# Softmax denominators of a cross-attention kernel: the context's share summed on TensorE, four rear pieces instead of five, a new order on every engine

## The reference, cut to what matters

```python
def layernorm(x, g, b): ...            # mean and variance over the last axis
def rmsnorm(x, gamma):
    norm = sqrt(sum(x * x)) * x.shape[-1] ** -0.5
    return x / maximum(norm, RMS_EPS) * gamma

# cross attention: x is (4, 512, 128), context (4, 77, 96), 2 heads of 64
lat = layernorm(_layernorm(x)); xn = layernorm(context)
q  = lat @ Wq.T
kv = concatenate([xn @ Wkv.T, lat @ Wlkv.T], axis=1)   # 77 context keys, then 512 of its own
attn = softmax(mask(rmsnorm(q) * SCALE @ rmsnorm(k).T))
x = x + (attn @ v) @ Wo.T + bo

# mixture of 8 experts, the best 2 of each token
l = _layernorm(x)
gates = softmax(l @ Wg + bg)
x = x + sum over the top 2 of gates * (l @ W[e] + b[e])
```

## Time and profile before

| what | value |
|---|---|
| median of three runs | 121.44 us (121.33 to 122.02) |
| profiled execution: time, span | 120.44 us, 118.6 us |
| PE busy | 105.5 us, 89% of the span |
| POOL busy | 92.3 us, 78% |
| ACT busy | 85.9 us, 72% |
| DVE busy | 79.4 us, 67% |
| PEld busy | 74.5 us, 63% |
| mean granted TensorE clock | 0.971 |

### The profile page before, as it was taken

One profiled execution on the slowest core, in us unless ns is written; L12 is line 12 of the kernel. 1 busy time (PEld: TensorE's weight loads), 2 busy tenths in 40 slices (PEclk: granted clock), 3 DMA queues, 4 the chain that ended last, 5 costly groups with the idle time before them and its releaser, 6 DMA issues.

```text
span 118.6 us, 2507 instructions
## 1 busy us (share of the span) xinstructions
PE 105.5 (89%) x733; PEld 74.5 (63%) x733; DVE 79.4 (67%) x317; ACT 85.9 (72%) x209; POOL 92.3 (78%) x113
## 2 busy tenths in 40 slices
PE   4999988999999989999999989999999999797500
PEld 4999877673487654654284577677578867485300
DVE  0541599302287572597209559999999999999990
ACT  0327878789898995799685799695969593597600
POOL 3570479999999999959986659949169899879982
PEclk9999998699999999999999999999999999999995
DMA  3616951000000000000000000000000110110112
GB/s 101 149 15 182 343 102 34 0 0 3 0 0 0 7 0 0 6 3 0 0 0 0 0 6 0 0 8 3 0 0 12 37 44 6 38 47 0 44 44 88
DMA packets 6679, 3.92 MB, mean 33 GB/s; under 512 B 2314, under 2 KB 6282, under 8 KB 6667
## 3 DMA queue, kind: packets, MB, share of 16 engines
q1 hardware_dynamic: 5835, 3.41, 10.4%
q10 hardware_dynamic: 832, 0.36, 1.1%
HBM read 2.72 MB, written 1.05 MB: 32 GB/s over the span
## 4 chain that ended last, share of the span: by engine, by line
POOL 38%; PE 27%; DVE 18%; issue 11%; ACT 3%; POOLq 1%; DVEq 0%; ACTq 0%
PE PS L923 8%; DVE part L892 6%; PE PS L1068 6%; POOL esum L421 5%; PE PS L1047 5%; POOL rq L396 4%; POOL e L430 4%; POOL xbo L442 4%; POOL rk L402 3%; POOL rstd L388 3%; PE PS L1102 2%; DVE acc L892 2%; POOL pair L473 2%; POOL rstd L450 2%; POOL We L378 2%
## 5 line engine op out<-in xcount | busy, mean ns | idle before, releaser
L602 ACT ACTIVATE probs<-PS,shift,rk 128x512 f32<-128x512 f32 (+1 forms) x40 | 25.0, 694 | 4.6 <-PE PS L1047 4.4
L660 ACT ACTIVATE scaled<-PS,w 128x128 f32<-128x128 f32 x64 | 17.4, 385 | 4.6 <-PE PS L916 3.7
L1068 PE MATMUL PS<-probs,V_sb 128*64 128x512 f32 (+1 forms) x80 | 16.1, 519 | 0.0
L914 PE MATMUL PS<-WeH,l2H 128*128 128x512 f32 x32 | 13.5, 423 | 1.8 <-ACT scaled L660 0.9
L473 POOL TENSOR_TENSOR pair<-scaled 128x512 f32<-128x512 f32 x8 | 10.3, 1286 | 4.0 <-ACT scaled L660 3.6
L916 PE MATMUL PS<-WeH,l2L 128*128 128x512 f32 x32 | 12.6, 393 | 0.0
L915 PE MATMUL PS<-WeL,l2H 128*128 128x512 f32 x32 | 12.5, 391 | 0.0
L430 POOL TENSOR_TENSOR e<-probs,probs 128x1024 f32<-128x1024 f32 (+1 forms) x5 | 9.7, 1931 | 3.0 <-ACT probs L602 3.0
L421 POOL TENSOR_TENSOR esum<-probs,probs 128x1024 f32<-128x1024 f32 (+1 forms) x5 | 10.7, 2141 | 1.1 <-ACT probs L602 1.1
L923 PE MATMUL PS<-ident 128*128 128x128 f32 x60 | 9.4, 324 | 1.5 <-POOL ident L366 1.5
L1047 PE MATMUL PS<-QH,KH 64*128 64x512 f32 (+1 forms) x40 | 9.0, 435 | 1.3 <-DVE QL L773 0.7
(11 more groups left out here) (144 smaller groups left out, 280.8 us busy)
## 6 DMA issues: line engine op xcount, KB each, us to landing
out_dram<-x SPq DMA_DIRECT2D x8, 128.0 KB, 1.7
x_sb<-in_x_dram SPq DMA_DIRECT2D x3, 256.0 KB, 5.5
We_sb<-in_L_ffn_W_dram SPq DMA_DIRECT2D x1, 512.0 KB, 5.3
We_end<-in_L_ffn_W_dram SPq DMA_DIRECT2D x1, 512.0 KB, 8.9
x_sb<-in_x_dram SPq DMA_DIRECT2D x2, 128.0 KB, 2.5
Wlkv_sb<-in_L_xattn_Wlkv_dram ACTq DMA_DIRECT2D x1, 128.0 KB, 3.0
ctx_sb<-in_ctx_dram SPq DMA_DIRECT2D x1, 115.5 KB
Wkv_sb<-in_L_xattn_Wkv_dram ACTq DMA_DIRECT2D x1, 96.0 KB, 2.8
```

The lines of the kernel that those rows point to most:

```text
L602: act.activation(probs[p % 2][n][:, h, s], ps[:, s], ACT.Exp, bias=shift[:, 0:1], scale=rk[:, b, n, h:h + 1]).then_inc(probs_made, 1)
L660: last = act.activation(scaled[m // 2 % 2][:, m % 2, e], ps[:, e], ACT.Copy, scale=w[:, m, e:e + 1])
L914: pe.matmul(dst, lH, rH, start=True, stop=False)
L1068: last = pe.matmul(bank("value", p, 0)[h * D:(h + 1) * D, s], v, pr, start=(n == 0), stop=(n == KT - 1))
```

## The change

It does six things.

1. `esum2` goes. `den` now has eight products: four with the sum of key tiles 0 to 3, and four with the context's 77 rows of `probs`, which accumulate into the same PSUM columns. `esum1` becomes `esum`. `den` waits for the context's exponentials itself, and the `exp` of piece p, for p from 2 on, also waits for the `den` of piece p-2, since that now reads the buffer.
2. `REAR` has four pieces: batch 3 is done whole.
3. The warm-up transposes go from 60 to 24 (14, 1, 4, 4, 1).
4. `logits_` reads the logits from PSUM for the difference `lgs`, and makes `two` by a reduction over one element instead of a copy.
5. `cbias_` works in the PSUM bank, without `mbias`.
6. All four tables are new: the order of the jobs on every engine and the banks.

```diff
-REAR = ((0, 0, 4), (1, 0, 4), (2, 0, 4), (3, 0, 2), (3, 2, 4))
+REAR = ((0, 0, 4), (1, 0, 4), (2, 0, 4), (3, 0, 4))
...
 TENSOR = """
-    warm 0 35 7   weights 0 0 0   warm 1 3 7   weights2 0 0 1   warm 2 11 7   xT 0 0 2   warm 3 11 7   q 0 0 3
+    warm 0 14 7   weights 0 0 0   warm 1 1 7   weights2 0 0 1   warm 2 4 7   xT 0 0 2   warm 3 4 7   q 0 0 3
...
                 if p >= 2 and n == 0:
 
                     act.wait_ge(O_done, p - 1)
+                    act.wait_ge(den_done, p - 1)
                     act.wait_ge(esum_made, p - 1)
...
-            def esum1_(p, n):
+            def esum_(p, n):
 
                 s = slice(0, (REAR[p][2] - REAR[p][1]) * P)
                 dve.wait_ge(e01_made, p + 1)
                 dve.wait_ge(e23_made, p + 1)
-                step(dve.tensor_tensor(esum[p % 2][:, :, s], esum[p % 2][:, :, s], e23[:, :, s], ALU.add))
-
-            def esum2_(p, n):
-
-                s = slice(0, (REAR[p][2] - REAR[p][1]) * P)
-                dve.wait_ge(dve_step, count[0])
-                dve.wait_ge(probs_made, H * KT * (p + 1))
-                dve.tensor_tensor(esum[p % 2][0:M, :, s], esum[p % 2][0:M, :, s], probs[p % 2][T][0:M, :, s],
-                                  ALU.add).then_inc(esum_made, 1)
+                dve.tensor_tensor(esum[p % 2][:, :, s], esum[p % 2][:, :, s], e23[:, :, s], ALU.add).then_inc(esum_made, 1)
...
-                dve.tensor_tensor(lgs[:, s], lg[:, s, 0:E], top[:, s, 0:1].to_broadcast([P, g, E]),
-                                  ALU.subtract).then_inc(lgs_made, 1)
-                dve.wait_ge(dve_step, step(dve.tensor_copy(two[:, s, 0:2], top[:, s, 0:2])))
+                dve.tensor_tensor(lgs[:, s], logits, top[:, s, 0:1].to_broadcast([P, g, E]), ALU.subtract).then_inc(lgs_made, 1)
+                dve.wait_ge(dve_step, step(dve.tensor_reduce(two[:, s, 0:2], top[:, s, 0:2].unsqueeze(3), AX.X, ALU.max)))
...
                 pe.wait_ge(esum_made, p + 1)
+                pe.wait_ge(probs_made, H * KT * (p + 1))
                 pe.wait_ge(consts_made, 2)
                 c = (e - a) * P // 2
                 for h in range(H):
                     for g in range(2):
                         r = slice((2 * h + g) * 32, (2 * h + g + 1) * 32)
-                        last = pe.matmul(bank("den", p, 0)[r, 0:c], ones[:], esum[p % 2][:, h, g * c:(g + 1) * c],
-                                         start=True, stop=True)
+                        pe.matmul(bank("den", p, 0)[r, 0:c], ones[:], esum[p % 2][:, h, g * c:(g + 1) * c],
+                                  start=True, stop=False)
+                for h in range(H):
+                    for g in range(2):
+                        r = slice((2 * h + g) * 32, (2 * h + g + 1) * 32)
+                        last = pe.matmul(bank("den", p, 0)[r, 0:c], ones[0:M], probs[p % 2][T][0:M, h, g * c:(g + 1) * c],
+                                         start=False, stop=True)
                 last.then_inc(den_done, 1)
```

More of the change, by code:

```diff
@@ new lines @@
+    warm 0 14 7   weights 0 0 0   warm 1 1 7   weights2 0 0 1   warm 2 4 7   xT 0 0 2   warm 3 4 7   q 0 0 3
+    k 0 0 4   xT 1 0 5   v 0 0 6   ctxT 0 0 7   warm 4 1 0   q 1 0 0   k 1 0 1   ctx_v 0 0 2   v 1 0 5
+    ctx_k 0 0 4   ssk 0 0 7   qT 0 0 6   qT 1 0 2   ctx_ss 0 0 5   maskT 0 0 3   ssk 1 0 0   score 0 0 74
+    score 0 1 62   score 0 2 53   score 0 3 01   score 0 4 47   xT 2 0 2   value 0 0 6   value 0 1 -
+    value 0 2 -   value 0 3 -   k 2 0 3   xT 3 0 5   q 2 0 0   v 2 0 1   q 3 0 2   k 3 0 4   v 3 0 7   den 0 0 5
@@ new lines @@
+    value 0 4 -   ssk 2 0 1   ssk 3 0 0   qT 2 0 3   xT 4 0 1   denT 0 0 7   qT 3 0 4   proj 0 0 65
+    score 1 0 20   score 1 1 13   v 4 0 4   q 4 0 0   k 4 0 2   score 1 2 13   score 1 3 56   value 1 0 7
+    value 1 1 -   score 1 4 13   score 2 0 56   qT 4 0 0   value 1 2 -   value 1 3 -   value 1 4 -   score 2 1 13
+    score 2 2 20   score 2 3 56   ssk 4 0 4   den 1 0 1   score 2 4 34   score 3 0 02   score 3 1 56   denT 1 0 1
+    value 2 0 7   value 2 1 -   value 2 2 -   value 2 3 -   value 2 4 -   proj 1 0 34   score 3 2 02
@@ new lines @@
+    score 3 3 56   den 2 0 7   proj 2 0 02   score 3 4 13   l2T 0 0 4   denT 2 0 5   value 3 0 6   value 3 1 -
+    value 3 2 -   gate 0 0 7   l2T 1 0 1   value 3 3 -   value 3 4 -   gate 1 0 3   proj 3 0 40   den 3 0 2
+    low 0 0 5   denT 3 0 1   low 0 1 7   low 0 2 6   low 0 3 2   low 1 0 3   l2T 2 0 5   high 0 0 7   high 0 1 0
+    high 0 2 1   high 0 3 4   low 1 1 6   low 1 2 2   low 1 3 3   gate 2 0 0   high 1 0 7   high 1 1 5
+    high 1 2 6   l2T 3 0 1   high 1 3 4   high 2 0 2   low 2 0 0   gate 3 0 1   low 2 1 5   low 2 2 7   low 2 3 3
@@ new lines @@
+    shift 0 0   ssq 1 0   stats1 2 0   qn 0 0   qn 1 0   msk 0 0   mask 0 0   ctx_kL 0 0   QL 0 0   QL 1 0
+    ctx_ms 0 0   cbias 0 0   msk 1 0   kL 1 0   stats1 3 0   stats1 4 0   esum 0 0   ssq 2 0   ssq 3 0
+    split 0 0   qn 2 0   kL 2 0   msk 2 0   kL 3 0   qn 3 0   msk 3 0   QL 2 0   QL 3 0   x2 0 0   ssq 4 0
+    stats2 0 0   qn 4 0   esum 1 0   kL 4 0   QL 4 0   msk 4 0   esum 2 0   x2 1 0   stats2 1 0   x2 2 0
+    stats2 2 0   logits 0 0   esum 3 0   top 0 0   logits 1 0   x2 3 0   stats2 3 0   top 1 0   high 0 0
@@ L849, in logits_ @@
                 dve.wait_ge(pads_made, 1)
[L850 to L852 removed]
+                logits = bank("gate", p, 0)[:, 0:g * E].rearrange("p (t e) -> p t e", e=E)
+                dve.wait_ge(dve_step, step(dve.tensor_copy(lg[:, s, 0:E], logits)))
                 for t in range(b * T + a, b * T + e):
```

82 lines of the change are left out of this document (27 added, 55 removed).

## The result

The kernel after takes 115.27 us, median of four runs (114.56 to 116.62); the kernel before, beside it, 121.56 (121.33 to 122.02). The ratio is 0.946, 95% interval 0.937 to 0.955. The forecast was 114.3, in a range of 110.3 to 119.3. Where its numbers are set against the forecast's, they are set against the profiled 113.3 and the span of 111.5.

What follows compares the result with a forecast made beforehand. TensorE was taken to become the bound in place of VectorE at the end: first score 16.0 + 45.4 + 2.9 + 39.1 + 2.7 + 5.4 = span 111.5 us, 7.1 less; profiled 113.3, median 114.3, range 110.3 to 119.3.

Steps and rivals of the forecast that it cites:

- The opening: Up to the first score: fewer unread transposes, weights' copy at about 5.1 us, first score at 16.0 instead of 18.9.
- The cost of the eight products: TensorE's `den`: the four added 77-row products cost between nothing and 0.57 us a piece; 0.57 was taken.
- GpSimd's additions: GpSimd's sums of exponentials: near 2.4 us each, where one took 3.42 beside VectorE's context addition.
- The stalls of the middle: TensorE, first score to x2 of batch 1: 2.9 us of stalls, 1.9 fewer, on 45.4 of work; x2 at 64.3.
- The first rival: Only the opening counts: GpSimd's full queue follows by 2.9 us only, x2 at 66.5, time 117.8 us; chance 0.17.
- The stalls behind x2: TensorE, x2 of batch 1 to its last product: half the stalls gone, 2.7 us left on 39.1 of work.
- The tail: Behind TensorE's last product: 5.4 us to the end of the span (0.3, 2.1 and 3.0), before 7.3.
- the rival of the other sign: TensorE's clock: fewer unread transposes leave 22 us at half clock against 3.5, 9.3 us more, 123.6 us; chance 0.08.

Runs made afterwards that it cites:

- e1: The kernel before with only the new warm-up counts (14, 1, 4, 4 unread transposes for 35, 3, 11, 11): 118.72 us, ratio 0.977.
- e2: The kernel after with the old warm-up counts (35, 3, 11, 11, 1): 118.81 us, ratio 0.964.
- e8: The kernel after with 20 more unread transposes on TensorE in its gap ahead of the key squares of batch 2: 113.42 us, ratio 0.933.
- e10: The kernel after, orders alone changed: `shifted` behind `xbo 2`, `split` behind `msk 4`, `kL 4` and `QL 4` ahead of `esum 1`: 111.58 us, ratio 0.914.
- e9: The kernel after with `lgs` reading the logits from SBUF and `two` made by a copy, as before: 114.60 us, ratio 0.943.
- e12: The kernel of e8 with the last batch's transposes and gate one expert half earlier: 113.04 us, ratio 0.927.
- e11: The orders of e10 with 8 unread transposes at the place of e8: 111.74 us, ratio 0.920.
- e5: The kernel before, in its old order, with the context's addition taken from VectorE and given to `den` as four more products: 121.32 us, ratio 0.996.
- e3: The kernel after with the context's 77-row addition back on VectorE and four products a `den`: 116.96 us, ratio 0.952.
- e13: As e8 with 10 unread transposes in place of 20: 113.30 us, ratio 0.933.

## Why the prediction was right, and where it was off

**The opening** was right in mechanism and nearly in size: the copy at 5.86 for 5.1, since the 14 transposes took 3.25 us and not 2.5, the first score at 16.28 for 16.0. The 2.5 was the mean of all 35, and the first ones are the slow ones: in before's own trace the window from 1.51 to 4.73 has 15 of them and the one from there to 7.71 has 22 (those on a border are counted twice), at a recorded clock of 1.00 in both. e1 and e2 show the step from both sides.

**The cost of the eight products.** A den of batch 1 runs from 58.22 to 59.23, 1.01 us for the 1.14 of the forecast. The 77-row products cost about as much as their neighbours: four of them take 0.55 us between starts and the others 0.46, and the means by form are 380 and 391 ns.

```profile
L1067 PE MATMUL PS<-esum,ones 128*32 128x256 f32 x32 | 2.6, 391 | 0.0
...
L1072 PE MATMUL PS<-probs,ones 77*32 77x256 f32 x32 | 2.5, 380 | 0.0
```

**GpSimd's additions** came out at 2.35 to 2.39 us each, none at 3.42 as in the earlier trace rows, as forecast.

**The stalls of the middle** are the term that was mis-sized: 2.9 forecast. From 16.28 to 67.49 are 51.2 us for 45.4 of work, so 5.8 of stalls. Nearly all of it is one place, 2.07 of idle and 3.4 from the half clock behind it. The prediction followed QL and xbo through the new tables, and not `shifted` and `split`, which the same tables had put ahead of the queries of batches 1 and 2. Without the half clock x2 comes at 64.29 (e8), with neither at 62.09 (e10). In e9, with after's tables, the stalls are 4.2 us, so 1.6 of the 5.8 belong to this one execution. The first rival forecast an x2 at 66.5, because GpSimd would be full. The time was near, but the cause was not that: GpSimd was busy for 43.1 of the 51.2 us, and in e10 it has the same jobs, and TensorE waited for it nowhere behind the identity at the start.

**The stalls behind x2** were over-sized: 2.7 forecast. 67.49 to 107.43 are 39.9 us for 39.1 of work, 0.8.

**The tail** was under-sized: 7.4 for 5.4. VectorE's end came 3.4 us after the last product, for 2.4; and from there to the end of the span were 4.0 us, for 3.0, since GpSimd still had two final additions to do, where before it had one. The sum took that 3.0 from before and had no term for GpSimd's queue. Window of 97 to 107 us in after, where VectorE is the third number behind the length and GpSimd the fifth:

```profile
97.00:107.00 10.00, 10.00 (x44) 7.83 (x44) 9.55 (x45) 8.14 (x32) 9.29 (x11) 1.00 0.09 29
```

By the mean over the whole stretch, 38.35 of 47.3, VectorE was no longer the bound, as forecast; in these ten microseconds it is nearly full, and so is GpSimd. That it is GpSimd which ends last shows in e9 as well: there VectorE's lag is 3.8 us, 0.4 more than in after, and the tail is 7.1. e10 has its last product ending at 101.61 and the same tail of 7.4, e12 7.0. What would shorten it was not tried beyond the gate's place.

Together: 0.3 for the opening, 2.9 for the middle, -1.9 behind it, 2.0 for the tail make 3.3, and the span is 114.8 for 111.5. The median was 1.0 above the forecast, since the other runs were faster than the profiled one, while the forecast had put the median 1.0 above the profiled one. So the mechanism held, but that the number came so near is in part luck: errors of 2.9 and 2.0 stand against one of 1.9 and against the median, which fell below the profiled time where it was put above.

**The clock** did fall, for 6.8 us in the profiled execution (3.4 in e9's) instead of 3.5, and behind the new gap, not at the first scores. It was the rival of the other sign, which needed 22 us, and e2 shows that more unread transposes in the opening do not prevent it: 0.86 from 18 to 30 us, 0.88 from 30 to 42.

## What to carry to other kernels

When an order is rewritten, go through every job that moved, those for a later stage above all: preparation for a later stage belongs where its engine idles, behind everything that the full engine will wait for. A gap of 2 us on TensorE cost 3.4 to 5.0 us here (49.6 and 51.2 us against the 46.2 of e10, which moved two more jobs), since the half clock came behind it; taking the wait away is best (e10), unread work in the gap wins about half of that while the wait stands (e8), and unread work where there is no gap is paid for (e11, and the 35 transposes of the opening). Taking work off an engine gains nothing by itself (e5, e9) until the order lets the full engine run ahead. When a wait for one engine shrinks, look at which engine is next at the end of the chain: here GpSimd took back at the end what VectorE had won.

## What the runs showed of the hardware

In these rows an addition on VectorE and one on GpSimd don't run side by side; one waits for the other. In e10 three rows of the two engines' timelines meet:

```profile
49.03 2.35 DVE L786 TENSOR_TENSOR esum<-esum,e 128x1024 f32<-128x1024 f32 x1
```

```profile
48.98 1.31 POOL L424 TENSOR_TENSOR xbo<-x_sb,bo_b 128x512 f32<-128x512 f32 x1
50.25 3.35 POOL L360 TENSOR_TENSOR We<-We_sb,We_end 128x1024 f32<-128x1024 f32 x1
```

VectorE's `esum` takes 1.23 alone. It stands until `xbo` ends at 50.25 and then needs 1.13 more; `shifted`, 2.37 alone, takes 3.35, about 1 us longer, as if it began near the time when `esum` ended, 51.38. In e3 the 77-row addition, 1.21 alone, began at 29.22 beside the same `shifted`, which ran to 30.24 in its usual 2.36: the addition ended at 31.31, 1.07 behind it. The Trainium skill, SBUF — State Buffer, "SBUF: two separate sides", describes it so: the pair of ports that both share is locked for a whole instruction, not divided. These rows agree, and 3.42 in the earlier trace rows is the same case.

The fall of the granted clock is not the same in every execution. The same tables gave 6.8 us at half in after and 3.4 in e9 behind the same wait, and e13 alone of the kernels with 14 transposes and after's tables had a fall at the first scores, from 16 to 19.5 us. Nor does the length of one idle decide it: behind an idle of 0.73 us (e2, at 37.6) the clock was at half from 39 to 42.5 us, and behind one of 1.67 us (e1, at 41.6) it stayed at 1.00.
